# Hard attention over a sparse graph: the score matmul split into eight 32-row matmuls, a joint minimum, and the owner matrix made by ScalarE

## The reference, cut to what matters

```python
# x: (4096, 256) f32; adj: (4096, 4096) int32; 8 heads of 32 columns
Q, K, V = per head of x @ WQ.T, x @ WK.T, x @ WV.T
attn = einsum('hqd,hkd->hqk', Q, K) * 32 ** -0.5 + (Q @ we.T + be)
attn = softmax(attn + where(adj > 0, 0, -inf), axis=-1)
hard = (attn == max(attn, axis=-1)).astype(f32) / 8     # one winner a row
out  = layernorm(x + einsum('hqk,hkd->hqd', hard, V))   # heads joined
```

## Time and profile before

| | us |
|---|---|
| median of 3 runs | 1331.66 (1328.04 to 1335.49) |
| the profiled execution's own time | 1323.72 |
| its span, first to last instruction | 1321.9 |

### The profile page before, as it was taken

One profiled execution on the slowest core, in us unless ns is written; L12 is line 12 of the kernel. 1 busy time (PEld: TensorE's weight loads), 2 busy tenths in 40 slices (PEclk: granted clock), 3 DMA queues, 4 the chain that ended last, 5 costly groups with the idle time before them and its releaser, 6 DMA issues.

```text
span 1321.9 us, 45630 instructions
## 1 busy us (share of the span) xinstructions
PE 1009.2 (76%) x12346; PEld 712.8 (54%) x12347; DVE 1017.9 (77%) x3019; ACT 818.9 (62%) x1483; POOL 735.1 (56%) x820
## 2 busy tenths in 40 slices
PE   5788468888778787778887787877877787778881
PEld 3334245565556555556555565655655565566561
DVE  6445457898879888878877888788888888888881
ACT  2423256677667677667756666676676676775661
POOL 0000156786767667656766656666556656656770
PEclk9998788999999999988988999999999989999995
DMA  4634576677686777677767777687778777866671
GB/s 164 230 120 151 164 237 223 201 218 257 193 253 204 250 254 236 202 236 243 225 206 252 233 238 228 199 274 265 241 258 269 247 256 259 261 208 189 211 215 34
DMA packets 89512, 290.93 MB, mean 220 GB/s; under 512 B 16984, under 2 KB 30040, under 8 KB 89496
## 3 DMA queue, kind: packets, MB, share of 16 engines
q0 software_dynamic: 48720, 199.60, 48.1%
q1 hardware_dynamic: 40776, 91.15, 20.9%
HBM read 275.98 MB, written 14.71 MB: 220 GB/s over the span
## 4 chain that ended last, share of the span: by engine, by line
PE 26%; DVE 23%; issue 18%; DMA 16%; DVEq 7%; POOL 4%; ACT 3%; POOLq 1%; SPq 0%; ACTq 0%
DMA kv<-kv_table,picks 14%; PE ps_s L1194 6%; DVE best L924 5%; PE ps_s L1213 5%; POOL kv L525 4%; PE ps_s L1130 3%; DVE picks L914 3%; PE ps_o L1225 2%; PE ps_r L1235 2%; DVE reached L895 2%; DVE hit L901 2%; PE ps_s L1120 2%; PE ps_h L1205 2%; DVE minus_top L929 2%; DVE o_all L941 2%
## 5 line engine op out<-in xcount | busy, mean ns | idle before, releaser
L525 POOL DMA_INDIRECT kv<-kv_table,picks x609 | 584.1, 959 | 332.6 <-PE ps_o L1225 181.4
L1194 PE MATMUL ps_s<-k_t,q_blk 128*128 128x384 f32 x804 | 363.8, 536 | 0.0
L639 ACT ACTIVATE hard<-ps_s,minus_top 128x384 bf16<-128x384 f32 x402 | 211.7, 579 | 138.4 <-DVE minus_top L929 130.1
L634 ACT COPY k_t<-ps_s 128x384 f32<-128x384 f32 x404 | 175.6, 483 | 161.9 <-PE ps_s L1213 161.6
L516 POOL TENSOR_TENSOR q_blk<-q_t,minus_same 128x256 f32<-128x256 f32 x202 | 149.6, 741 | 222.3 <-issue 156.5
L1213 PE MATMUL ps_s<-ident_f,kv 128*128 128x128 f32 x1212 | 182.4, 290 | 74.4 <-DMA kv<-kv_table,picks 73.8
L924 DVE TENSOR_REDUCE best<-ps_s 128x1 f32<-128x384 f32 x402 | 204.6, 546 | 28.1 <-PE ps_s L1196 19.5
L624 ACT ACTIVATE hard_t<-ps_h 128x768 bf16<-128x768 bf16 x200 | 162.0, 810 | 68.5 <-PE ps_h L1205 59.2
L1205 PE MATMUL ps_h<-ident_b,hard 128*128 128x128 bf16 x1200 | 104.1, 225 | 116.1 <-ACT hard L639 115.8
L1196 PEld LDWEIGHTS ps_s<-mask_of,masked 128*128 128x128 bf16 x1206 | 104.3, 101 | 152.6 <-issue 102.8
L1213 PEld LDWEIGHTS ps_s<-ident_f,kv 128*128 128x128 f32 x1212 | 139.3, 149 | 86.3 <-DMA kv<-kv_table,picks 76.5
(11 more groups left out here) (137 smaller groups left out, 1132.1 us busy)
## 6 DMA issues: line engine op xcount, KB each, us to landing
adj_in<-in_adj SPq DMA_DIRECT2D x128, 512.0 KB, 5.8
kv_table<-kv_out SPq DMA_DIRECT2D x32, 320.0 KB, 2.6
kv<-kv_table,picks POOLq DMA_INDIRECT x609
x_in<-in_x SPq DMA_DIRECT2D x8, 512.0 KB, 6.6
x_row<-in_x SPq DMA_DIRECT2D x32, 128.0 KB
out<-y_out SPq DMA_DIRECT2D x32, 128.0 KB
plan<-places_of SPq DMA_DIRECT2D x212, 0.0 KB
turn_flags<-flags_of SPq DMA_DIRECT2D x53, 0.0 KB
```

What stands on the lines that cost most here:

```text
L525: pool.indirect_dma_start(kv[m % RING][:, c, :], None, kv_table, bass.IndirectOffsetOnAxis(ap=picks[m % RING][:, c, 2:3], axis=0)).then_in ...
L634: act.copy(k_t[m % 2][:, h, :], ps_s[m % 2][h][:, 0:SLOTS]).then_inc(act_kt[h], 1)
L639: done = act.activation(hard[m % 2][:, h, :], ps_s[m % 2][h][:, 0:SLOTS], ACT.Sign, bias=minus_top[m % 2][:, h:h + 1], scale=-1.0)
L1194: pe.matmul(bank[:, 0:SLOTS], q_blk[m % 2][:, h, :], k_t[m % 2][:, h, :], start=True, stop=False)
```

## The change

1. `scores` is called once an item, ahead of `hards_across(b)`. The two 128-row float32 matmuls are replaced by eight of 32 rows and 32 columns of the array, one for each head: head j of half h is read at partitions 32 j and written at partitions 32 ((j + h) mod 4), so each of the eight uses another 32 x 32 part of the array. They all stand ahead of the six mask matmuls. `values` and the last matmul of the output undo the rotation of half 1 (`ident_8` is longer by 32 columns).
2. POOL copies 32 queries (`q_now`, ring of 4) instead of making the block diagonal; it waits for the scores of item b - 2 in place of b. The minus sign moves into the key rows of the table (L806).
3. The two score banks of an item are one buffer of two banks, and DVE takes both minima in one instruction once both halves are there.
4. `owners` moves from DVE to ACT, between `hard_rows` and `keys`, as a Sign with a bias from `edge_of` (+1 or -1 in place of 0 or 1). The constants `differ` and `pay` are halved and wrapped round to fit. PE waits for `act_reached`, and also for `dve_vals` of the item before, ahead of `planes_of`; ACT waits for `pe_planes` two items back, and walks the item list itself.

```diff
-            def blocks_of_q(m, due, at):
+            def queries(m, due, at):
                 if due is not None:
-                    wait_alone(pool, pe_score[1], due(pe_score[1], -2))
-                pool.tensor_tensor(q_blk[m % 2][:].rearrange("p a (h q) -> p a h q", h=HEADS4),
-                                   q_t[:, :, bass.ds(at, GQ)].unsqueeze(2).to_broadcast([P, HALVES, HEADS4, GQ]),
...
+                    wait_alone(pool, pe_score[1], due(pe_score[1], -RING))
+                pool.tensor_copy(q_now[m % RING][:], q_t[:, :, bass.ds(at, GQ)]).then_inc(q_made, 1)
...
+            def owners(m, due, k="at"):
+                at = act.snap(r[k], min_val=0, max_val=TABLES * GPT * 16 - 1)
+                act.wait_ge(pe_planes, due(pe_planes, -2))
+                act.activation(reached[m % 2][:], iota_h[:], ACT.Sign,
+                               bias=edge_of[:].rearrange("p g i -> p (g i)")[:, bass.ds(at, 1)]
+                               ).then_inc(act_reached, 1)
...
                     masks(b + 2, for_loop(act, r, 2))
                     hard_rows(b, for_loop(act, r, 0))
+                    owners(b + 5, for_loop(act, r, 5), f"ahead{b + 5}")
                     for h in range(HALVES):
                         keys(b + 2, for_loop(act, r, 2), h)
...
-                                         scalar=SCALE, in1=we_sb[:], op0=ALU.mult, op1=ALU.add).then_inc(k_done, 1)
+                                         scalar=-SCALE, in1=we_sb[:], op0=ALU.mult, op1=ALU.subtract).then_inc(k_done, 1)
...
-                for h in range(HALVES):
-                    dve.wait_ge(pe_score[h], due(pe_score[h]))
-                    done = dve.tensor_reduce(best[:, h:h + 1], ps_s[m % 2][h][:, 0:SLOTS], AX.X, ALU.min)
-                done.then_inc(dve_best, 1)
+                dve.wait_ge(pe_score[0], due(pe_score[0]))
+                dve.wait_ge(pe_score[1], due(pe_score[1]))
+                dve.tensor_reduce(best[:], ps_both[m % 2][:, :, 0:SLOTS], AX.X, ALU.min).then_inc(dve_best, 1)
...
+            def scores(m, due):
+                pe.wait_ge(dve_k, 12)
+                pe.wait_ge(q_made, due(q_made))
+                pe.wait_ge(act_kt[1], due(act_kt[1]))
+                for j in range(HEADS4):
+                    for h in range(HALVES):
+                        to, head = (j + h) % HEADS4 * HD, j * HD
+                        pe.matmul(ps_s[m % 2][h][to:to + GQ, 0:SLOTS], q_now[m % RING][head:head + HD, h, :],
+                                  k_t[m % 2][head:head + HD, h, :], start=True, stop=False)
+                for h in range(HALVES):
+                    bank = ps_s[m % 2][h]
+                    for c in range(CHUNKS):
+                        mm = pe.matmul(bank[:, c * P:(c + 1) * P],
+                                       masked[m % RING][:, c, :, :].rearrange("p h q -> p (h q)"), mask_of[:],
+                                       start=False, stop=(c == CHUNKS - 1))
+                    mm.then_inc(pe_score[h], 1)
...
-                    scores(b + 1, for_loop(pe, r, 1), 0)
+                    scores(b + 1, for_loop(pe, r, 1))
                     hards_across(b, for_loop(pe, r, 0))
-                    scores(b + 1, for_loop(pe, r, 1), 1)
```

More of the change, by code:

```diff
@@ L162, in hard_attention @@
         kv = [sb(f"kv{i}", [P, CHUNKS, ROW], F32) for i in range(RING)]
-        q_blk = [sb(f"q_blk{i}", [P, HALVES, P], F32) for i in range(2)]
+        q_now = [sb(f"q_now{i}", [P, HALVES, GQ], F32) for i in range(RING)]
         k_t = [sb(f"k_t{i}", [P, HALVES, SLOTS], F32) for i in range(2)]
@@ L602, in flags_back, with walk @@
                 act.copy(flag_t[:], ps_flag_t).then_inc(act_flag_t, 1)
+            r = registers(act, ("n", "left", "it", "g", "next", "at") + TURN + tuple(places("ahead", 5)),
+                          n=BASE, left=1, fe=FIRST_TILES, fin=FIRST_TILES, due=PLANNED)
+            def walk():
+                next_item(act, r)
+                act.reg_alu(r["at"], r["g"], TABLES * GPT - 1, ALU.bitwise_and)
+                act.reg_alu(r["at"], r["at"], 4, ALU.logical_shift_left)
+                act.reg_add(r["at"], r["at"], r["it"])
+            def owners(m, due, k="at"):
[4 more added lines that the diff above has]
+                               ).then_inc(act_reached, 1)
             x_copy(0, 0)
@@ L614, in _ @@
                         value_mid(g * GT + j - 1)
+                if 3 <= g <= 7:
+                    act.wait_ge(dve_fin, FIN * ((g - 3) // 4) + LISTED_ENDS)
+                    walk()
+                    owners(g - 3, for_item(g - 3))
                 if g % 2 == 0 and g // 2 < FIRST_TILES:
@@ L685, in take_plan @@
                 plan_made(act, r)
+                load_places(act, r, LISTED, places("ahead", 5))
                 next_turn(act, r)
@@ L763, in _ @@
             dve.wait_ge(dve_k, 3)
+            dve.scalar_tensor_tensor(out=differ[:], in0=ident_f[:], scalar=0.5, in1=wraps[:], op0=ALU.mult,
+                                     op1=ALU.add)
             dve.tensor_scalar(weigh[:], weigh_f[:], power_row[:].bitcast(F32), None, ALU.mult)
@@ L1151, in ranks @@
             def ranks(f1, fin0, read):
-                pe.wait_ge(dve_reached, read) if read is not None else None
+                pe.wait_ge(dve_vals, read) if read is not None else None
                 pe.wait_ge(act_flag_t, f1)
@@ L1185, in planes_of @@
                         if c == 0 and i == 0:
-                            mm._wait_ge(dve_reached, due(dve_reached))
+                            mm._wait_ge(act_reached, due(act_reached))
                 mm.then_inc(pe_planes, 1)
[L1189 to L1198, removed]
+            def scores(m, due):
[14 more added lines that the diff above has]
+                    mm.then_inc(pe_score[h], 1)
             def hards_across(m, due):
@@ L1283, in _ @@
                 keys_across(m, for_item(m), 48, m)
-            for h in range(HALVES):
-                scores(0, for_item(0), h)
+            scores(0, for_item(0))
             def turn():
```

73 lines of the change are left out of this document (34 added, 39 removed).

## The result

| | us | ratio to before (95% interval) |
|---|---|---|
| before, 4 runs | 1329.85 (1325.15 to 1335.49) | |
| after, 4 runs | 1311.91 (1308.77 to 1318.0) | 0.9866 (0.9839 to 0.9893) |
| after, measured again beside later runs (6 runs) | 1313.77 (1308.07 to 1322.04) | 0.9871 (0.9844 to 0.9897) |

The change makes the kernel 1.3% faster, about 18 us; the forecast was 52 us. The direction was right, the size three times too large.

A forecast was written before the change was run, and what follows sets the result against it. No one engine was taken to bound the loop; DVE, PE with ACT, and gathers with POOL shared it. Savings of 13, 31 and 8 us took 1323.7 to 1272, with the median 8 us above: 1280 us, own range 1240 to 1315, wider 1240 to 1460.

The forecast's parts named there:

- The eight matmuls side by side: TensorE scores: the eight small matmuls overlap in full, 0.85 us against 1.4, saving PE 0.5 us an item; chance 46%.
- Strict order: Rival on TensorE: second record of each small matmul holds back the whole queue, 3.1 us an item, 1432 us; chance 28%.
- no overlap: Rival on TensorE: parts sharing rows or columns exclude each other, or float32 does not run so; 1870 us; chance 16%.
- ScalarE: ACT gains `owners`, about 0.6 us, and goes from 3.8 to 4.3 us an item, under the item's 5.59.
- GpSimd: POOL's query copy takes 0.25 us against 0.73 for `q_blk`; 8 us in all from items held by gathers and POOL.
- joint minimum: On DVE, one minimum over 768 elements takes 0.95 us against 1.01 for both halves, 0.07 saved an item.
- PE's feared wait for the key copies: On TensorE after `values` and `planes_of`: up to 0.7 us an item unless front-end work lies there; costed at nothing.
- VectorE: DVE saves 0.17 us an item, 0.1 of it from `owners` moving away; 13 us over the 75 items DVE holds.
- Order of half 1: TensorE: half 1's scores ahead of `hards_across` fill PE's idle time; up to 0.87 us an item, half taken, 31 us.
- Table and constants: The sign in L806, halved constants and longer `ident_8`: same instructions or one more at the start, under 1 us, nothing.
- The sum: Whole kernel: 13 us from 75 DVE items, 31 from 72 PE and ACT items, 8 from 53 gather and POOL items: 52 us.
- The third rival: Gain not felt: the gather loop or ACT's 2.3 us replaces the removed wait, PE waits longer for rows; 1332 us; chance 10%.

The follow-up runs named there:

- e2: The kernel before with one edit: on TensorE the scores of half 1 go ahead of `hards_across`; 1345.75 us, ratio 1.0154.
- short rows: Each gather fetches only the key row, 256 of 640 words, output without V; changed kernel 0.9454, kernel before 0.9816.
- f4: The changed kernel with short rows plus eight unread bf16 matmuls ahead of the key transposes in three of four steps; 1259.16 us, ratio 0.9459.
- f3: The changed kernel with eight unread bf16 matmuls ahead of the key transposes in three of four steps, measured again; 1302.56 us, ratio 0.9788.

## Why the prediction was wrong in size

- *The eight matmuls side by side*: shown, 0.80 us to the first mask matmul for a forecast 0.85. Strict order and no overlap, which had 44% of the chance, are excluded by the 0.80 us. `values` had been the right row to read.
- *ScalarE, GpSimd, the joint minimum*: prices right within 2%. PE's feared wait for the key copies is 6.6 us in the whole run. What the joint minimum and POOL's earlier wait are worth was not measured.
- *VectorE*: `owners` away from DVE gives 1.0%, 13 us for a forecast of 8 for that part. Right in kind; the interval, 0.4 to 1.6%, holds the 8 us too.
- *Order of half 1*: costed as up to 0.87 us gained per item held by PE, taken as half, 31 of the 52 us. On the kernel before it costs 1.5% (e2), since half 1 had covered `hard_rows`: the cover of a wait was moved and its price was not asked. What it is worth in the changed kernel, where the joint minimum needs it, stays open.
- *Table and constants*, costed at nothing: the loop starts 5.7 us later. Profiles with `owners` on DVE start it at 179.4 to 182.6 us, those with it on ACT at 182.3 to 189.0. How much of it is ACT's place in the front end and how much varies from run to run is not separated.
- *The sum*: this is the step that failed. Shares of the chain were turned into 72, 75 and 53 items and each kind was credited with its own saving, as if an item that DVE or PE no longer holds would come sooner. It comes only as soon as its rows do: PE waits for rows in 81 stretches, before in 62, and for 102.2 us in place of 76.5. The short rows show what this costs: the same change gives 3.7% with short rows and 1.3% with full ones. That 3.7% lies close to the forecast 3.9% is luck, since the forecast's largest term was the order, and what paid with short rows was in good part the small matmuls, 1.7%.
- *The third rival*, given 10%, is what happened to about two thirds of the gain (1.3% of 3.7% is left). Its argument against was DMA at 0.73. That was a mean over the loop: in the landing of 7.15 us the share is 0.92, in the longer half of all such stretches 0.94, and there is little room.
- *The clock*, which no rival named, fell from 0.96 to 0.90 in the loop. Filler that raised it gave back 0.8%. This is not a loss beside the late rows: with short rows a higher clock gave nothing (f4).

## What to carry to other kernels

Shares of a chain are not a budget in which each engine's saving counts by its share. A mean DMA share is no proof of room either: look at the share in the stretches in which rows are late. Before summing, write down each loop that closes over several items (here: buffer freed, gather issued, rows landed, transposes, values) with its length per item, and cap every gain at the next longest. When work is moved, ask which wait it had been covering. And when TensorE is relieved, look at the granted clock: idle time can cost the work behind it.

## What the runs showed of the hardware

- Eight 32 x 32 float32 matmuls of 384 columns, 16 records, took 0.87 us, and one wide float32 matmul 0.86 us. The first records of all eight started within 0.05 us, the second ones 0.34 us later. Calls of four, two an item, took 345.7 / 402 = 0.86 us each, calls of eight 200.4 / 201 = 1.00 us on average.
- Adding 150 groups of eight bf16 matmuls (94 us of PE time by their line in f3) made the kernel 0.8% faster while the granted clock rose from 0.880 to 0.943.
- Of the stretches from the last gather to the transposes that waited for it, the longer half averaged 6.5 us at a DMA share of 0.94, the shorter half 4.7 us at 0.77 (profile after).
